# Two LSTM layers on one core: the gate transpose in three parts, the second layer 19 steps behind

## The reference, cut to what matters

```python
x = x + L0(x, cond)          # layer norm, low-rank weights per batch, one product
x = x + L1(x, cond)          # tanh(x @ W_ih.T + h_term)
def lstm(x, h0, Wx, Wh, b):  # L2, then L3 on L2's sum
    xp = x @ Wx + b                                  # for all steps
    def step(h, c, xp_t):
        i, f, o, g = split(xp_t + h @ Wh)            # sigmoid, sigmoid, sigmoid, tanh
        c = f * c + i * g
        h = o * tanh(c)
        return h, c
```

## Time and profile before

| | us |
|---|---|
| median of 3 runs (11978.43 to 11982.7) | 11978.62 |
| profiled execution | 11984.53 |
| its span, first to last instruction | 11982.7 |
| TensorE busy | 11879.4 |
| VectorE busy | 8271.9 |
| ScalarE busy | 3084.4 |
| GpSimd busy | 1421.3 |

### The profile page before, as it was taken

The page is one execution under the profiler, slowest core; times in us unless marked ns, Lnnn a source line. Parts: engine busy times, 40 slices in busy tenths (PEclk is TensorE's granted clock), DMA queues, the critical chain, the costliest instruction groups (busy, mean ns, idle before and its releaser), DMA issues.

```text
span 11982.7 us, 420395 instructions
## 1 busy us (share of the span) xinstructions
PE 11879.4 (99%) x231988; PEld 2758.3 (23%) x100916; DVE 8271.9 (69%) x34054; ACT 3084.4 (26%) x20602; POOL 1421.3 (12%) x5238
## 2 busy tenths in 40 slices
PE   8999999999999999999999999999999999999998
PEld 5222222222222222222222222222222222222222
DVE  2577777777777777777777777777777777777765
ACT  2222222222222222222222222222222222222221
POOL 4011111111111111111111111111111111111110
PEclk9999999999999999999999999999999999999999
DMA  4000000000000000000000000000000000000000
GB/s 163 24 4 5 4 4 5 5 4 5 5 4 4 5 4 4 5 4 4 5 4 5 5 4 4 5 4 4 5 4 4 5 4 4 5 4 4 4 5 3
DMA packets 374421, 106.86 MB, mean 9 GB/s; under 512 B 349594, under 2 KB 357830, under 8 KB 372436
## 3 DMA queue, kind: packets, MB, share of 16 engines
q1 hardware_dynamic: 362372, 61.96, 2.8%
q0 software_dynamic: 3504, 11.56, 0.3%
q10 hardware_dynamic: 6560, 6.32, 0.2%
HBM read 62.98 MB, written 16.78 MB: 7 GB/s over the span
## 4 chain that ended last, share of the span: by engine, by line
PE 95%; DVE 3%; issue 1%; ACT 1%; DVEq 0%; POOLq 0%; POOL 0%
PE bank L80 86%; PE bank L874 7%; DVE gates_t L1053 1%; PE bank L518 1%; PE bank L531 1%; DVE pre L1058 0%; ACT gate_if L945 0%; ACT tanh_c L951 0%; DVE g_c L1067 0%; DVE state L1076 0%; DVE state L1080 0%; DVE g_fc L1062 0%; DVE state L1083 0%; PE bank L484 0%; DVE turned L1022 0%
## 5 line engine op out<-in xcount | busy, mean ns | idle before, releaser
L80 PE MATMUL bank<-wh,state 128*6 128x512 bf16 x196608 | 11320.6, 379 | 55.5 <-DVE state L1083 44.9
L1053 DVE STREAM_TRANSPOSE gates_t<-bank 128x512 f32<-128x512 f32 x4096 | 2937.8, 717 | 976.0 <-PE bank L80 972.6
L80 PEld LDWEIGHTS bank<-wh,state 128*6 128x6 bf16 x65536 | 1558.6, 85 | 6431.8 <-issue 6262.9
L945 ACT ACTIVATE gate_if<-pre 128x16 f32<-128x16 f32 x4096 | 894.8, 218 | 7565.6 <-DVE pre L1058 7565.6
L1076 DVE TENSOR_TENSOR state<-gate_o,tanh_c 128x8 f32<-128x8 f32 x4096 | 690.2, 169 | 1124.2 <-ACT tanh_c L951 1028.6
L1062 DVE TENSOR_TENSOR g_fc<-gate_if,g_c 128x8 f32<-128x8 f32 x4096 | 689.1, 168 | 782.6 <-ACT gate_if L945 782.6
L951 ACT ACTIVATE tanh_c<-g_c 128x8 f32<-128x8 f32 x4096 | 854.9, 209 | 1101.6 <-DVE g_c L1067 1101.6
L1058 DVE TENSOR_REDUCE pre<-gates_t 128x24 f32<-128x96 f32 x4096 | 1036.8, 253 | 139.5
L982 POOL TENSOR_TENSOR x<-x1r,state 128x8 f32<-128x8 f32 x2048 | 436.5, 213 | 5461.8 <-DVE state L1083 5461.8
L982 POOL TENSOR_TENSOR y<-x,state 128x8 f32<-128x8 f32 x2048 | 436.1, 213 | 4948.5 <-DVE state L1083 4948.5
L1067 DVE TENSOR_TENSOR_SCAN g_c<-gate_if,g_fc 128x16 f32<-128x16 f32 x4096 | 784.2, 191 | 155.8 <-DVE g_fc L1062 17.9
(11 more groups left out here) (120 smaller groups left out, 1690.4 us busy)
## 6 DMA issues: line engine op xcount, KB each, us to landing
w<-in_w SPq DMA_DIRECT2D x8, 2048.0 KB, 11.6
out<-y_rows SPq DMA_DIRECT2D x1020, 8.0 KB, 1.8
wx<-in_x SPq DMA_DIRECT2D x16, 512.0 KB, 5.1
x1p<-x_t_all SPq DMA_DIRECT2D x128, 64.0 KB, 2.6
x1r<-x_t_all SPq DMA_DIRECT2D x128, 64.0 KB, 2.6
x_t_all<-wx ACTq DMA_DIRECT2D x6, 1024.0 KB, 4.8
wx<-in_Wh POOLq DMA_DIRECT2D x8, 512.0 KB, 4.3
wx<-in_Wh POOLq DMA_DIRECT2D x16, 256.0 KB, 4.4
```

The costliest lines, as they stand in the source:

```text
L80: return pe.add_instruction(mybir.InstMatmult(name=nc.get_next_instruction_name(), engine=mybir.EngineType.PE, ins=[pe.lower_ap(moving), p ...
L945: act.activation(gate_if[l][:, :, :, 1], pre[l][:, 0:2 * HB].rearrange("p (w n) -> p w n", w=2), ACT.Sigmoid).then_inc(S[l]["if"], 1)
L1053: dve.transpose(gates_t[l][:, :, NS * NB:], gates[l][:, 0:NMS * C].rearrange("p (m c) -> p m c", c=C)).then_inc(s["trans"], 1)
```

## The change

The transpose of a step is done in three parts: 256 columns (i and f), 128 (g), 128 (o). The sum is done in three parts as well, each after its transpose; the o sum stands behind f*c. The wait for the copied projection (`xp`) moves from the transpose to the first sum. ScalarE does the sigmoid of f, then that of i, as two instructions, and f*c waits for f's alone; tanh of g waits for the g sum. The waits of h change places. LAG becomes 19 and SUMS deals the projection sets out anew: 8 sets in each of the steps 0 and 1 of a chunk (all of L3), 2 in steps 2 and 3, one in steps 4 to 15 (all of L2). ROWS_AT follows from LAG and becomes 4.

```diff
-SUMS = ((0,) * 8 + (2,) * 8, (2,) * 8 + (0,) * 8)
-LAG = CH + 8 + 1
+SUMS = ((0, 0, 2, 2) + (1,) * 12, (8, 8) + (0,) * 14)
+LAG = CH + 2 + 1
...
 # ScalarE
-act.wait_ge(S[l]["pre"], n)
-act.activation(gate_if[l][:, :, :, 1], pre[l][:, 0:2 * HB].rearrange("p (w n) -> p w n", w=2),
-               ACT.Sigmoid).then_inc(S[l]["if"], 1)
+act.wait_ge(S[l]["pre_if"], n)
+act.activation(gate_if[l][:, 1, :, 1], pre[l][:, HB:2 * HB], ACT.Sigmoid).then_inc(S[l]["f"], 1)
+act.activation(gate_if[l][:, 0, :, 1], pre[l][:, 0:HB], ACT.Sigmoid)
+act.wait_ge(S[l]["pre_g"], n)
 act.activation(g_fc[l][:, :, 0], pre[l][:, 2 * HB:3 * HB], ACT.Tanh).then_inc(S[l]["g"], 1)
...
 # VectorE
-ifg = 3 * NH // NS
-dve.wait_ge(s["xp"], n)
-dve.wait_ge(s["mm"], n)
-dve.transpose(gates_t[l][:, :, NS * NB:],
-              gates[l][:, 0:NMS * C].rearrange("p (m c) -> p m c", c=C)).then_inc(s["trans"], 1)
-dve.wait_ge(s["trans"], n)
-dve.tensor_reduce(sums[:, 0:ifg], terms[:, 0:ifg], AXX, ALU.add).then_inc(s["pre"], 1)
-dve.tensor_reduce(sums[:, ifg:], terms[:, ifg:], AXX, ALU.add).then_inc(s["pre_o"], 1)
-dve.wait_ge(s["if"], n)
+gf, ifg = 2 * NH // NS, 3 * NH // NS
+banked = gates[l][:, 0:NMS * C].rearrange("p (m c) -> p m c", c=C)
+dve.wait_ge(s["mm"], n)
+dve.transpose(gates_t[l][:, 0:gf, NS * NB:], banked[:, 0:gf]).then_inc(s["trans_if"], 1)
+dve.transpose(gates_t[l][:, gf:ifg, NS * NB:], banked[:, gf:ifg]).then_inc(s["trans_g"], 1)
+dve.wait_ge(s["trans_if"], n)
+dve.wait_ge(s["xp"], n)
+dve.tensor_reduce(sums[:, 0:gf], terms[:, 0:gf], AXX, ALU.add).then_inc(s["pre_if"], 1)
+dve.wait_ge(s["trans_g"], n)
+dve.tensor_reduce(sums[:, gf:ifg], terms[:, gf:ifg], AXX, ALU.add).then_inc(s["pre_g"], 1)
+dve.transpose(gates_t[l][:, ifg:, NS * NB:], banked[:, ifg:]).then_inc(s["trans_o"], 1)
+dve.wait_ge(s["f"], n)
 dve.tensor_tensor(g_fc[l][:, :, 1], gate_if[l][:, 1, :, 1], g_c[l][:, :, 1],
                   ALU.mult).then_inc(s["fc"], 1)
+dve.wait_ge(s["trans_o"], n)
+dve.tensor_reduce(sums[:, ifg:], terms[:, ifg:], AXX, ALU.add).then_inc(s["pre_o"], 1)
...
+dve.wait_ge(s["tanh"], n)
 dve.wait_ge(s["res"], n)
-dve.wait_ge(s["tanh"], n)
```

More of the change, by code:

```diff
@@ L733, in blocks_of @@
             return [(NFRONT + n // (2 * NH), n // NH % 2, n % NH) for n in units]
-        names = ("mm", "xp", "trans", "pre", "pre_o", "if", "g", "fc", "c", "tanh", "h", "r1", "r2", "res",
+        names = ("mm", "xp", "trans_if", "trans_g", "trans_o", "pre_if", "pre_g", "pre_o", "f", "g", "fc", "c", "tanh", "h", "r1", "r2", "res",
                  "proj", "turn", "ready")
@@ L1048, in emit @@
                                 "p m (k b) -> p m b k", b=NS * NB)[:, :, :, ::-1]
-                            ifg = 3 * NH // NS
-                            dve.wait_ge(s["xp"], n)
-                            dve.wait_ge(s["mm"], n)
-                            dve.transpose(gates_t[l][:, :, NS * NB:],
-                                          gates[l][:, 0:NMS * C].rearrange("p (m c) -> p m c", c=C)
-                                          ).then_inc(s["trans"], 1)
-                            dve.wait_ge(s["trans"], n)
-                            dve.tensor_reduce(sums[:, 0:ifg], terms[:, 0:ifg], AXX, ALU.add).then_inc(s["pre"], 1)
-                            dve.tensor_reduce(sums[:, ifg:], terms[:, ifg:], AXX, ALU.add).then_inc(s["pre_o"], 1)
-                            dve.wait_ge(s["if"], n)
+                            gf, ifg = 2 * NH // NS, 3 * NH // NS
[4 more added lines that the diff above has]
+                            dve.wait_ge(s["trans_if"], n)
+                            dve.wait_ge(s["xp"], n)
+                            dve.tensor_reduce(sums[:, 0:gf], terms[:, 0:gf], AXX, ALU.add).then_inc(s["pre_if"], 1)
[3 more added lines that the diff above has]
+                            dve.wait_ge(s["f"], n)
                             dve.tensor_tensor(g_fc[l][:, :, 1], gate_if[l][:, 1, :, 1], g_c[l][:, :, 1],
                                               ALU.mult).then_inc(s["fc"], 1)
+                            dve.wait_ge(s["trans_o"], n)
+                            dve.tensor_reduce(sums[:, ifg:], terms[:, ifg:], AXX, ALU.add).then_inc(s["pre_o"], 1)
                             dve.wait_ge(s["fc"], n)
```

## The result

The changed kernel takes **11899.22 us** (median of 4 runs, 11897.58 to 11900.64) against 11980.66 (4 runs, 11978.43 to 11983.34): ratio 0.9932, 95% interval 0.9918 to 0.9947. That is 81.4 us less. The forecast was 60 less (11919), its range 11893 to 11955: the direction and the range were right, the size was a quarter short. The profiled execution took 11900.05, its span is 11898.2.

The account below looks back on a forecast made before the run. TensorE was taken to bound the kernel, with 0.09 us to spare over the chain. Lag, chain and end terms gave -45.0 us, stalls -15, sum -60: timed median 11919 us, range 11893 to 11955.

Parts of the forecast that it names:

- What bounds: Middle of the run: TensorE bounds with 26 waves, 5.617 us a step, against the chain's cycle of 5.525; 0.09 to spare.
- Rival 2: Twelve one-set steps a chunk: the chain shortens by less than the 0.13 us needed; with 0.05, 12064 us; chance 9%.
- sign of being wrong: Light steps above 5.42 us with TensorE idle until the last remainder, 1512 times; or single steps still above 5.40.
- The chain: From recurrent matmuls to the next state: split transpose and moved waits take 0.30 us off each chain; cycle 5.22.
- Rival 1: VectorE's instructions stand end to end once three transposes and three sums mix: cycle 5.72, total 12415 us; chance 3%.
- Rival 5: Waits in the chain: moving them does nothing; gain 0.17 us, cycle 5.355, total 11936; chance 8%.
- Lag and sums: Step schedule: 12 single steps go, 6 double ones come, -32.6 us; redealt projection sets change TensorE's sum by 0.
- The stalls: VectorE instructions late without late data, mostly absorbed by light steps' spare time: -15 us, bounds +10 and -40.
- rival 4: Steps with both layers and one projection set absorb all stalls: -45 - 40, total 11894 us; chance 10%.

Follow-up runs that it names:

- quarters turned at once: Changed kernel, but in steps with one layer finished quarters are turned after the same step's second remainder, not the next step's scan: 11895.79 us, ratio 0.9929.

## Why the prediction was right, and where it was short

- **What bounds.** Right, and the sharpest test of it came out: 25 waves hold at 5.398 as long as the chain's cycle is below (5.19, 5.13, 5.33, 5.39), and with the old chain the light steps follow the chain at 5.53. Rival 2's point of decision, 5.395, is confirmed from both sides. The sign of being wrong, idle time of TensorE before 1512 blocks, did not come: its recurrent matmuls stand idle for 20.8 us in the whole run.
- **The chain.** 0.337 instead of 0.304 off the cycle. Links of transposes and waits came out within 0.02; the rest is small: the i/f sums took 0.18 and not 0.215. The 256-column transpose took 0.45 (0.44 forecast). Of the 0.337, the moved waits are 0.14 (5.525 to 5.39), the split 0.26 (5.39 to 5.13 with the joint sigmoid), and the sigmoid of f -0.06. I had booked f first inside the split without pricing its order against g's: a loss that I did not name.
- **Rival 1**, VectorE's instructions end to end, is refuted: the transposes start 0.37 and 0.20 apart at 0.45 and 0.28 of duration. By the prediction's own sum it would have made the kernel some 440 us slower than before. The prediction put this rival beside "VectorE: DVE Perf Modes", section "The DRAIN you can't avoid", of the Trainium skill, and read only half of that section. The same section also says that a next operation that is not held starts earlier; the wish for few operations stands in another one, "Rules for kernel authors". The starts here agree with the half that was left out, and 12 instructions for 9 made the chain shorter.
- **Rival 5**, moved waits that do nothing, is refuted by the two that were put back. (Its total was also added wrongly: -45 + 5 gives 11939, not 11936.)
- **Lag and sums**: L3 alone to the end gave -36.9 for -38.9. Missing in the forecast were the wait for a turned quarter in step 1 (1.15) and the slow step at the start of chunk 128 (1.7). The argument that I used, that each half of a heavy step has 16 waves and the two alternating buffers are free in time, does not hold with one layer, where all 8 sets stand in one step and their turns wait for the next. In chunk 1 likewise, and there the clock's slow step moved in from the end of chunk 0: -1.9 there, +1.7 here.
- **The stalls** are the term that was mis-sized: -15 forecast, -36.5 measured (bound -40), which is more than the whole miss (from the first step on 79.8 less, where 60 was forecast). What happened is rival 4, the light steps absorb nearly all stalls, to which the prediction gave 10%: its 11894 is 5 us from the measured time, the forecast's 11919 is 20. The range held because it took rival 4 in. Four things were off. The spare time is 0.21, not 0.17. Late instructions did not grow by a third as VectorE's instructions did; they fell from 136 to 57, 55 of the 79 with h's wait order (late h's and first remainders), 18 with the split (late scans), which the prediction did not see. A late scan, 0.36, lengthens its step by at most 0.17 in the changed kernel, and only 31 of 1984 steps are long there, the one at the loop's end included. And some 4 us are the loop's turns and its end, which the prediction counted among the small stalls. That "at least 0.1" us would be to spare where a projection's weight loads stand in front was given without a row, and no run shows it.
- **Luck.** The profiled execution before had 4.2 us of stall and slow clock at the loop's end and an idle stretch at the tail without a fall of the clock; the changed one had 0.9 and a fall (1.7). These few us do not change the account.

## What to carry to other kernels

- An engine that is 99% busy can hide a dependence cycle that is 1.6% shorter than its own. Measure that cycle where it stands alone (one layer, no filler) before dealing work out anew; here the same new order costs 177 us with the old chain and gains with the new one.
- With 0.09 us to spare, nearly all of a stall of 0.2 to 0.36 us is paid. Giving the chain 0.2 us of room, and an order of waits with fewer late instructions, was worth some 32 us without any change to the bounding work.
- Of two waits before one instruction, list the late one first, and do not put an instruction in front of the one that the join waits for last.

## What the runs showed of the hardware

- A wait listed second and late costs about 0.07 us: 0.07 in h alone (5.525 to 5.455), 0.14 in two places (5.19 to 5.33).
- VectorE's late instructions stand a whole multiple of 128 of its instructions apart within a round of the loop, in the kernel before (256, 384, 384, 640, ...), with h's order alone (512, 512, 1408, 256, ...) and in the changed kernel (3456, 2176, 896, 128, ...), waits and register operations counted; these rows are scans and first remainders. They cost 0.19 behind h and 0.32 to 0.36 before the scan and before h, and nothing where the engine waits anyway.
- They go with the supply of instructions. The profile has a DMA queue of kind "instruction" whose packets are of 8192 bytes (packets, MB, share; before and changed kernel):

```profile
q14 instruction: 672, 5.51, 0.1%
...
q14 instruction: 800, 6.55, 0.2%
```

  In the kernel before, the next packet of this queue starts 1.0 us (median; 0.86 to 1.30 for nine in ten) after the time at which a late instruction was due; after a VectorE instruction picked at random it is 11.6 us in the median. With h's order alone and in the changed kernel it is 1.0 us as well. That ties the stalls to the fetch of blocks; why a block's first instruction is late in some places of the text and on time in others is not shown.
- Where the loop's text starts again or ends, VectorE stood still for up to 2.6 us (before, 11489.5 to 11492.1). The steps there were late by 0.9 us in all in the changed kernel, 1.9 in the one with the shorter chain alone, 5 in the kernel before.
- An idle stretch of 2.4 us of TensorE was followed by 3.4 us at half the clock, 1.2 instead of 2.4 GHz, in the changed kernel at 11791.7, and cost its step 1.7 us. With filler matmuls before it did not come. At the tail of the eleven profiles without filler the idle stretch was 2.4 to 2.8 us; the clock fell after it in eight and not in three (before, 2.77; only the waits moved, 2.62; quarters turned at once, 2.42). The length of the idle stretch does not decide it; what does stays open.
